# The opening of a gated cross-attention and expert kernel: order of loads, normalisation and mask rows

## What is computed

```python
x = x + tanh(g_xattn[0]) * xattn(layernorm(x), ctx_1024, Wq, Wk, Wv, Wo, bo)
x = x + tanh(g_ffn[0]) * ffn(layernorm(x), gate_w, w_gate, w_up, w_down)
```

## Time and profile before

| | |
|---|---|
| median of 3 runs | 1925.38 us (1925.32 to 1926.35) |
| the profiled execution | 1929.9 us, its span 1928.1 us |
| mean granted TensorE clock | 0.976 |
| TensorE busy (matmul) | 1781.3 us, 92% of the span |
| VectorE, ScalarE, GpSimd busy | 1112.6, 871.7, 922.4 us |

### The profile page before, as it was taken

How to read it: one execution, slowest core, us unless ns; L and a number is a source line. 1 busy time by engine, 2 the same in 40 slices (tenths; PEclk the granted TensorE clock), 3 DMA queues, 4 the chain that set the end, 5 groups by cost and what they waited for, 6 DMA issues and landing times.

```text
span 1928.1 us, 41223 instructions
## 1 busy us (share of the span) xinstructions
PE 1781.3 (92%) x13350; PEld 1052.6 (55%) x13414; DVE 1112.6 (58%) x2777; ACT 871.7 (45%) x1684; POOL 922.4 (48%) x963
## 2 busy tenths in 40 slices
PE   3799999999999999963899999999999999999997
PEld 1355555555555555531456565655655665656565
DVE  2678888888888888736743434343434344343431
ACT  1356555665655655632343434343334334343332
POOL 4467777777777776544143332424232424233322
PEclk9799999999999999986999999999999999999999
DMA  6676777777777776439365673645646645445222
GB/s 150 155 166 165 182 184 186 186 186 186 185 181 183 186 183 153 118 93 230 82 112 88 120 124 86 103 88 102 111 68 127 117 84 101 86 87 89 50 32 24
DMA packets 411285, 247.66 MB, mean 128 GB/s; under 512 B 293271, under 2 KB 392735, under 8 KB 411167
## 3 DMA queue, kind: packets, MB, share of 16 engines
q1 hardware_dynamic: 386591, 212.53, 47.6%
q0 software_dynamic: 24576, 33.57, 11.0%
HBM read 118.63 MB, written 58.72 MB: 92 GB/s over the span
## 4 chain that ended last, share of the span: by engine, by line
PE 49%; DVE 2%; SPq 1%; DMA 1%; issue 1%; POOL 1%; ACT 0%; POOLq 0%
PE bank L1090 11%; PE bank L1089 11%; PE bank L1091 10%; PE bank L1107 6%; PE bank L1106 6%; PE bank L1105 6%; SPq L1016 1%; DMA gate_raw<-in_L_ffn_w_gate 1%; DVE h L1207 0%; DVE h L1210 0%; ACT h L1135 0%; SPq L995 0%; DVE top_at L1157 0%; POOL gate_nat L1034 0%; POOL up_nat L1034 0%
## 5 line engine op out<-in xcount | busy, mean ns | idle before, releaser
L1055 POOL DMA_INDIRECT out<-y,row_now x128 | 202.0, 1578 | 604.7 <-ACT y L1142 580.0
L579 ACT ACTIVATE prob<-bank 128x512 f32<-128x512 f32 x640 | 367.6, 598 | 230.2 <-PE bank L472 146.7
L1207 DVE TENSOR_TENSOR h<-bank,silu 128x512 f32<-128x512 f32 x256 | 176.3, 689 | 395.7 <-PE bank L1091 262.8
L662 DVE CUSTOM_DVE_ANT_0 masked<-bank,causal 128x384 bf16<-128x384 f32 (+1 forms) x512 | 300.4, 616 | 51.5 <-PE bank L449 49.5
L1135 ACT ACTIVATE h<-h 128x512 bf16<-128x512 f32 x256 | 161.7, 632 | 345.7 <-DVE h L1207 330.1
L449 PE MATMUL bank<-ks,qs 96*128 96x128 bf16 (+3 forms) x1024 | 277.1, 306 | 37.2 <-DVE mx L662 15.1
L1210 DVE TENSOR_TENSOR h<-h 128x512 bf16<-128x512 f32 x256 | 177.3, 693 | 179.9 <-ACT h L1135 176.3
L1107 PE MATMUL bank<-downT,h 128*128 128x256 bf16 x1024 | 279.1, 273 | 0.0
L1105 PE MATMUL bank<-downT,h 128*128 128x256 bf16 x1024 | 279.1, 273 | 0.0
L1106 PE MATMUL bank<-downT,h 128*128 128x256 bf16 x1024 | 279.1, 273 | 0.0
L1090 PE MATMUL bank<-tokT,gateT 128*128 128x512 bf16 x511 | 194.7, 381 | 35.2 <-DMA tokT<-rows 29.1
(11 more groups left out here) (144 smaller groups left out, 2832.7 us busy)
## 6 DMA issues: line engine op xcount, KB each, us to landing
q_parts<-q_sb SPq DMA_DIRECT2D x64, 192.0 KB, 2.9
k_parts<-k_sb SPq DMA_DIRECT2D x64, 192.0 KB, 3.3
qs<-q_parts SPq DMA_DIRECT2D x64, 192.0 KB, 3.0
ks<-k_parts SPq DMA_DIRECT2D x64, 192.0 KB, 3.3
x_t<-in_x SPq DMA_DIRECT2D x16, 512.0 KB, 3.9
ctx_t<-in_ctx SPq DMA_DIRECT2D x16, 512.0 KB, 4.7
qs<-q_parts SPq DMA_DIRECT2D x64, 128.0 KB, 2.9
ks<-k_parts SPq DMA_DIRECT2D x64, 128.0 KB, 3.3
```

The source lines that it names most:

```text
L579: nc.scalar.activation(prob[:, gr % 2, h0:h0 + nh, POFF[tiles[0]]:POFF[tiles[0]] + w], sc_bank[SC_BANK[k]][:, 0:nh * w].rearrange("p (h w) ...
L662: nc.vector.tensor_tensor_reduce(masked[:, k % 2, 0:w], max_bank[max_at(gr, k)][:, 0:w], causal[:, T - w:T], 1.0, LOWEST, ALU.add, ALU.max ...
L1055: nc.gpsimd.indirect_dma_start(out_rows, bass.IndirectOffsetOnAxis(ap=row_now[:, par, c, s:s + 1], axis=0), y[:, c % 2, s, :], None, compu ...
```

## The change

Five things change place or size.

- SP loads x and the context of batch 0 first, wq after them.
- The two gate scalars and `bo` are loaded by ScalarE's own DMA queue, at its start.
- VectorE normalises batch 0 (`ln1+`) before the weights' remainders; the piece is left out of the rounds for batch 0.
- GpSimd makes the tails before the reciprocal deviation, each four tiles wide (512 columns instead of 128).
- SP copies the tails out behind batch 0's key stack of group 1, in pieces of 512 columns; its wait for the tails moves there too. GpSimd's wait for the bias moves to the residual of batch 0.

```diff
--- before.py
+++ after.py
@@ -210,7 +210,7 @@
     rest = sb(ctx, "rest", [P, 2, T], F32)
     qs = sb(ctx, "qs", [P, GROUPS, GH, T], BF16)
     ks = sb(ctx, "ks", [P, GROUPS, GH, T], BF16)
-    tail_of = {n: sb(ctx, f"{n}_tail", [P, P], BF16) for n in ("q", "k")}
+    tail_of = {n: sb(ctx, f"{n}_tail", [P, NT, P], BF16) for n in ("q", "k")}
     prob = sb(ctx, "prob", [P, 2, GH, PALL], F32)
     v_new = sb(ctx, "v_new", [P, NT, D], F32)
     v_aug = sb(ctx, "v_aug", [P, NT, HEADS, 32], F32)
@@ -369,6 +369,12 @@
                         sp.dma_start(to[at:at + rows, gr, :, :].rearrange("p h t -> p (h t)"), src)\
                             .then_inc(stack_loaded[gr], 16)
                         at += rows
+                    if n == "k" and gr == 1 and isinstance(b, int) and b == 0:
+                        sp.wait_ge(tails_made, 6)
+                        for tail, full, first in (("q", qs, ROWS), ("k", ks, STACK)):
+                            dst = full[first:P, :, :, :].rearrange("p g h t -> p (g h) t")
+                            sp.dma_start(dst, tail_of[tail][first:P, :, :].rearrange("p j c -> p (j c)").unsqueeze(1)
+                                         .broadcast_to([P - first, GROUPS * GH, T])).then_inc(tails, 16)
                 elif kind == "mrow":
                     gr = p[2]
                     n = count(b, GROUPS, gr)
@@ -390,19 +396,10 @@
             def load_weights(n):
                 sp.dma_start(w_raw[n][:, :, :], g[n].rearrange("(o p) i -> p o i", p=P)).then_inc(w_loaded[n], 16)
 
-            load_weights("wq")
             load(0)
-            for n in ("wk", "wv", "wo"):
+            for n in ("wq", "wk", "wv", "wo"):
                 load_weights(n)
             sp.dma_start(gw_raw[:, :], g["gate_w"]).then_inc(w_loaded["gate_w"], 16)
-            sp.dma_start(bo_rep[:, :], g["bo"].partition_broadcast(P)).then_inc(gates_loaded, 16)
-            sp.dma_start(gates[:, 0:1], g["g_xattn"].partition_broadcast(P)).then_inc(gates_loaded, 16)
-            sp.dma_start(gates[:, 1:2], g["g_ffn"].partition_broadcast(P)).then_inc(gates_loaded, 16)
-            sp.wait_ge(tails_made, 6)
-            for n, to, first in (("q", qs, ROWS), ("k", ks, STACK)):
-                dst = to[first:P, :, :, :].rearrange("p g h (j c) -> p (g h j) c", c=P)
-                sp.dma_start(dst, tail_of[n][first:P, :].unsqueeze(1).broadcast_to(
-                    [P - first, GROUPS * GH * NT, P])).then_inc(tails, 16)
             rounds(sp, piece)
             sp.wait_ge(x1_stored, 16 * BATCH)
             sp.wait_ge(tok_stored, 16 * BATCH)
@@ -547,6 +544,9 @@
 
         @block.scalar
         def _(act):
+            act.dma_start(gates[:, 0:1], g["g_xattn"].partition_broadcast(P)).then_inc(gates_loaded, 16)
+            act.dma_start(gates[:, 1:2], g["g_ffn"].partition_broadcast(P)).then_inc(gates_loaded, 16)
+            act.dma_start(bo_rep[:, :], g["bo"].partition_broadcast(P)).then_inc(gates_loaded, 16)
             act.wait_ge(gates_loaded, 48)
             nc.scalar.activation(tanh_g[:, :], gates[:, :], ACT.Tanh).then_inc(tanh_done, 1)
             for n, (name, o) in enumerate(order):
@@ -743,6 +743,8 @@
             nc.vector.tensor_copy(identb[:, :], ident[:, :]).then_inc(cast, 1)
             piece(-1, ("ln1", 0, 0))
             piece(-1, ("ln1", 0, 1))
+            piece(-1, ("ln1+", 0, 0))
+            piece(-1, ("ln1+", 0, 1))
             for n, (name, o) in enumerate(order):
 
                 dve.wait_ge(hi_taken, n + 1)
@@ -755,7 +757,13 @@
             dve.wait_ge(gates_loaded, 48)
             dve.wait_ge(tanh_done, 1)
             nc.vector.tensor_scalar(bias[:, :], bo_rep[:, :], tanh_g[:, 0:1], None, ALU.mult).then_inc(bias_done, 1)
-            rounds(dve, piece)
+
+            def later(body, p):
+                if p[0] == "ln1+" and isinstance(p[1], int) and p[1] == 0:
+                    return
+                piece(body, p)
+
+            rounds(dve, later)
 
         @block.gpsimd
         def _(pool):
@@ -800,6 +808,8 @@
                                             op=ALU.subtract).then_inc(split_lo["y"], 1)
                 elif kind == "res":
                     wait(pool, res_loaded, count(b, 16, 16))
+                    if isinstance(b, int) and b == 0:
+                        pool.wait_ge(bias_done, 1)
                     nc.gpsimd.tensor_tensor(out=res_t[:, :, :], in0=res_t[:, :, :],
                                             in1=bias[:, :].unsqueeze(1).broadcast_to([P, NT, D]),
                                             op=ALU.add).then_inc(res_done, 1)
@@ -842,23 +852,22 @@
                                     base=0, pattern=[[-1, P]], channel_multiplier=1).then_inc(consts, 1)
 
             pool.wait_ge(consts, CONSTS)
-            piece(-1, ("ln1", 0, 1))
-            nc.gpsimd.memset(tail_of["q"][:, :], 1.0).then_inc(tails_made, 1)
-            nc.gpsimd.memset(tail_of["k"][:, :], 0.0).then_inc(tails_made, 1)
+            nc.gpsimd.memset(tail_of["q"][:, :, :], 1.0).then_inc(tails_made, 1)
+            nc.gpsimd.memset(tail_of["k"][:, :, :], 0.0).then_inc(tails_made, 1)
             pool.wait_ge(tails_made, 2)
-            nc.gpsimd.affine_select(out=tail_of["k"][:, :], in_=tail_of["k"][:, :], compare_op=ALU.is_ge, fill=NEG,
-                                    base=-1 - SUB * (STACK + 1), pattern=[[-1, P]], channel_multiplier=SUB)\
+            nc.gpsimd.affine_select(out=tail_of["k"][:, :, :], in_=tail_of["k"][:, :, :], compare_op=ALU.is_ge, fill=NEG,
+                                    base=-1 - SUB * (STACK + 1), pattern=[[0, NT], [-1, P]], channel_multiplier=SUB)\
                 .then_inc(tails_made, 1)
-            nc.gpsimd.affine_select(out=tail_of["q"][:, :], in_=tail_of["q"][:, :], compare_op=ALU.is_ge, fill=0.0,
-                                    base=SUB * ROWS, pattern=[[1, P]], channel_multiplier=-SUB)\
+            nc.gpsimd.affine_select(out=tail_of["q"][:, :, :], in_=tail_of["q"][:, :, :], compare_op=ALU.is_ge, fill=0.0,
+                                    base=SUB * ROWS, pattern=[[0, NT], [1, P]], channel_multiplier=-SUB)\
                 .then_inc(tails_made, 1)
             pool.wait_ge(tails_made, 4)
-            nc.gpsimd.memset(tail_of["k"][STACK:ROWS, :], 1.0).then_inc(tails_made, 1)
+            nc.gpsimd.memset(tail_of["k"][STACK:ROWS, :, :], 1.0).then_inc(tails_made, 1)
             pool.wait_ge(tails_made, 5)
-            nc.gpsimd.affine_select(out=tail_of["q"][:, :], in_=tail_of["q"][:, :], compare_op=ALU.is_ge, fill=0.0,
-                                    base=-1 - SUB * (STACK + 1), pattern=[[-1, P]], channel_multiplier=SUB)\
+            nc.gpsimd.affine_select(out=tail_of["q"][:, :, :], in_=tail_of["q"][:, :, :], compare_op=ALU.is_ge, fill=0.0,
+                                    base=-1 - SUB * (STACK + 1), pattern=[[0, NT], [-1, P]], channel_multiplier=SUB)\
                 .then_inc(tails_made, 1)
-            pool.wait_ge(bias_done, 1)
+            piece(-1, ("ln1", 0, 1))
             rounds(pool, piece)
```

## The result

| | before | changed |
|---|---|---|
| median, 10 runs each | 1928.33 us (1925.32 to 1931.71) | 1922.29 us (1919.18 to 1924.33) |
| ratio, 95% interval | | 0.9968 [0.9957, 0.9978] |
| the profiled execution, its span | 1929.9, 1928.1 | 1922.38, 1920.7 |

Faster by 6.0 us, by the interval 4.2 to 8.3, where 9.1 was forecast. The time itself, 1922.29, lies above the range of 1914.0 to 1919.5, and 6.0 above the forecast of 1916.3. The other half is lead that was won and lost again.

The account below looks back on a forecast made before the run. TensorE, busy in its written order from the third slice on, was taken as the bound; -9.16 us for the opening and 0 for tail copies and smaller moves made -9.1, from 1925.38 to 1916.3 us, range 1914.0 to 1919.5.

Parts of the forecast that it names:

- The opening: Before the first query product: weight and x chains run side by side, moving it from 28.10 to 18.94, 9.16 us earlier.
- rival (a): First twelve query products: a warm TensorE runs them at the key products' pace, about 1.4 us remain, 1914.9; chance 0.12.
- tanh was to run before 7: ScalarE's tanh in the opening, at 10.49 before: running before 7 was a sign that the forecast was right.
- The tail copies: SP's copies behind group 1's key stack: hidden in 8 us of room, cost zero, at the high end 0.5 us.
- the new pieces are 1 KB, like those of the fast row, so I take the middle, over by about 49: Pace of SP's tail copies: between 135 GB/s (over at 51.8) and 382 GB/s (over at 47).
- rival (b): Tail copy at its old pace or slower takes 1 to 2.5 us from the next x transpose: 1918; chance 0.08.
- The value is not critical ... I take zero: Gates on ScalarE's queue: landing up to 4.7 us earlier or no earlier, either way zero cost or gain.
- A microsecond saved before the first score work reaches the end unless something takes it back: From the third slice on TensorE works through its written order, so the opening's saving of 9.16 us counts in full.
- rival (c): Full clock returns no earlier than before, giving back up to half the lead: 1920.8; with a second stretch 1923 to 1925; chance 0.08.
- limit 14: Sign of being wrong: a transposed x for batch 1 more than 14 us behind the group 0 start.
- limit 61: Sign of being wrong: a half clock on TensorE that lasts past 61 us.

Follow-up runs that it names:

- e1: The kernel before with only the four-tile-wide tails and their late copies behind group 1's key stack; ratio to before 0.9997.
- e4: The changed kernel with the two gate scalars and the bias loaded by SP again, behind the weights; ratio to before 0.9949.
- e8: The changed kernel with gates and bias back on SP and the q tail's copy moved behind batch 0's context transpose; ratio to before 0.9948, median 1918.86 us.
- e2: The changed kernel with the q tail's copy moved behind batch 0's context transpose, only the k tail's left behind group 1; ratio to before 0.9951.
- e11: The changed kernel with six products of 512 columns on constant tiles in TensorE's wait for batch 1's transposed x; ratio to before 0.9954.
- e13: The kernel before with only the three small loads (gates and bias) moved to ScalarE's queue at its start; ratio to before 1.0001.
- e0: The changed kernel itself, profiled and timed once more without any edit; ratio to before 0.9966.
- e5: The changed kernel with 45 products on constant tiles in TensorE's idle stretch before group 0's first maximum product; ratio to before 0.9968.
- e9: The changed kernel reordered: wq first, tanh last, two remainders before normalisation, narrow tails copied early, gates on SP, batch 1's context load later; ratio to before 0.9953.
- e3: The changed kernel with tails one tile wide again, copied in 256-byte pieces at the same late place; ratio to before 0.9956.

## Why the prediction was right or wrong

**The opening: right, step by step.** Power at 8.56 (8.5 forecast), normalisation 9.65 (9.6), first split 10.45 (10.47), first remainder 11.25 (11.27), first query product 18.97 (18.94). The mechanism, two chains that had stood one behind the other, is the measured one; group 0 gained another 0.7, the twelve query products taking 4.18 us instead of 4.85 (a third of the 1.9 that the pace of rival (a), 0.24 each, would have saved). One sign missed here: tanh was to run before 7 and ran at 8.88, without cost.

**The tail copies: no cost shown, size wrong.** Zero was taken, and in the wait they cost nothing (e1; e4 against e8); in time e2 leaves it open. But "the new pieces are 1 KB, like those of the fast row, so I take the middle, over by about 49" was wrong: they had landed at 44.00 + 8.2 = 52.2, at 178 GB/s against 144 in small pieces, so piece size is worth a quarter and not the factor of nearly three to 382. The 1 to 2.5 us of rival (b) were an estimate that no run shows: the copies had landed 1.3 us after batch 1's x transposes were issued, and in e1, where they landed 1.7 us after, the wait was 1.19 against 1.23. Whether the number of partitions sets the pace no run shows, since none copied to more.

**"The value is not critical ... I take zero", of the gates on ScalarE's queue: wrong.** I had asked only when the gates land. What they do to the large loads beside them wasn't in the sum: the issue of wk 1.3 us longer, wq 1.6 later, x late by 1.7 and 3.2 us in two executions (e11, e13). In the changed kernel's own opening that cost nothing: the first query product came at 18.97, with them on SP at 18.92 (e8) and 19.35 (e4). Whether it costs time isn't shown: e4 and e8 were 3.6 us faster, and so, within 0.6, was e2 with them on ScalarE.

**"A microsecond saved before the first score work reaches the end unless something takes it back": the step that failed.** The sum has -9.16 for the opening and nothing taken back. Two things took it. The wait for batch 1's x grew by 1.43, of which about 0.8 goes with an instruction load between its transposes; I had only the tail copies as a suspect. And 2.31 went in the stages with half clock (0.65 in six query products; 1.66 behind them, where six keys at 2.50 instead of 1.46 alone make 1.04): rival (c), given 0.08, named it, but priced another course. The full clock came back 7 us earlier and not 9.8, and a second half-clock stretch followed. 9.83 - 1.43 - 2.31 = 6.09, the lead at batch 2's load in the trace; e0 repeats it. Two of the prediction's own signs of being wrong came up: batch 1's transposed x was used 14.19 us behind group 0's start (limit 14), and half clock lasted to 62.9 (limit 61). What placed the instruction load and the second stretch, and the last 0.7 of the wait, stays open.

That the medians differ by 6.0 too is partly luck: the lead went on to 5.4 at batch 15 and 7.4 at the end of the profiled pair, and the interval is 4.2 to 8.3.

**The base.** The forecast was made on 1925.38; ten runs give 1928.33. A lead of 9.1 on that would be 1919.2, and a lead of 6.0 on 1925.38 would be 1919.3: either miss alone would have stayed inside the range of 1914.0 to 1919.5, and both together left it. The profiled execution, 4.5 above the median of three, was a sign that three runs were too few.

## What to carry to other kernels

When chains run one after the other, list which of them needs nothing from the other, and check both ends after the move: the time is set by whichever comes last, here to a tenth of a microsecond of what the rows gave (18.97 against 18.94). Then follow the lead through the first steady batches; here the stages with half clock (2.31 us) and a longer wait for batch 1's x (1.43, about 0.8 of it with an instruction load between the transposes) took 3.74 of 9.83. Look at where a filler ends as well as at what it fills: with the 45 products of e5 the clock stayed at 1.00 to their end at 41.2, and in the 3.14 us pause behind them it fell to 0.50. And before giving a variant credit for 3 us, look for another variant without the edit that is as fast.

## What wasn't expected of the hardware

- Three loads of 0.5 to 128 KB on ScalarE's queue at the start went with a longer issue of wk on SP's in every trace (1.43 to 2.32 us instead of 0.47 to 0.51), and in two of the eight kernels that have them so x came 1.7 and 3.2 us later.
- A 16 KB instruction load between two transposing DMAs goes with an issue of 3.9 us instead of 2.7 (the changed kernel, e0, e2; 3.36 in e9).
- Forty-four products of 512 columns in a row left the clock full until 2.5 us into the pause behind them, where it fell to half (e5: products to 41.2, half from 43.7, next product at 44.30).
- Copies from 30 and 32 partitions to the same ran at 178 GB/s in pieces of 1 KB and at 144 (e3) and 135 in pieces of 256 bytes.
